# Message pass of a graph transformer block: the routing of a batch cut into eight parts over eight steps, token and gate copied per ring run, low one-hots first in VectorE's step and places last

## The reference

```python
xn = layernorm(x)
# graph attention: a softmax over the edges of each source, summed at each destination
z = leaky_relu(xn @ W_s.T [src] + xn @ W_t.T [dst]);  e = z @ W_attn.T
alpha = exp(e - m[src]) / denom[src]
agg = segment_sum(xn[src] * alpha, dst);  gnn = agg @ W_fc.T + b_fc
# linear attention over all nodes: one 64x64 matrix per head from keys and values
mix = (q @ (instance_norm(k).T @ instance_norm(v)) / N) @ w_out.T + b_out
x = x + gnn + mix
# mixture of experts, 8 experts, one expert per token, capacity C = ceil(1.25 * T / 8)
h = layernorm(x);  probs = softmax(h @ gate_w + gate_b);  idx = argmax(probs);  prb = max(probs)
pos = (running count of idx up to this token) - 1;  kept = pos < C
y = expert_mlp[idx](h) * (prb * kept);  x = x + y
```

## Time and profile before

| | us |
|---|---|
| median of 3 runs (lowest, highest) | 2184.84 (2179.74, 2191.25) |
| span of the profiled execution | 2181.3 |
| PE / DVE / ACT / POOL busy in it | 1899.4 / 1486.4 / 781.6 / 1223.5 |
| first `window_sums` of the message pass starts | 1212.19 |
| `window_sums` of step 97 starts | 1710.65 |

### The profile page before, as it was taken

The page is one execution under the profiler, slowest core; times in us unless marked ns, Lnnn a source line. Parts: engine busy times, 40 slices in busy tenths (PEclk is TensorE's granted clock), DMA queues, the critical chain, the costliest instruction groups (busy, mean ns, idle before and its releaser), DMA issues. The chain is left out here.

```text
span 2181.3 us, 44890 instructions
## 1 busy us (share of the span) xinstructions
PE 1899.4 (87%) x12055; PEld 1346.6 (62%) x12055; DVE 1486.4 (68%) x6582; ACT 781.6 (36%) x3785; POOL 1223.5 (56%) x1251
## 2 busy tenths in 40 slices
PE   8997888878888888888887899999999679999997
PEld 5654555545555545555544566666666479999996
DVE  7775788878887888788787587666767624343433
ACT  6772444444444444444443011111111123333332
POOL 0006777777777777777774576656766312222222
PEclk9997889889888899899898799889999789999998
DMA  7867888888888888888885898877978566565650
GB/s 238 245 220 208 254 243 253 248 242 242 254 245 241 251 247 250 241 253 250 246 253 165 249 313 264 266 234 254 323 245 259 157 242 200 195 202 191 204 186 28
DMA packets 287974, 507.17 MB, mean 233 GB/s; under 512 B 59024, under 2 KB 199730, under 8 KB 287580
## 3 DMA queue, kind: packets, MB, share of 16 engines
q1 hardware_dynamic: 212556, 279.91, 40.8%
q0 software_dynamic: 75152, 224.23, 34.3%
HBM read 394.78 MB, written 112.83 MB: 233 GB/s over the span
## 5 line engine op out<-in xcount | busy, mean ns | idle before, releaser
L836 POOL DMA_INDIRECT pool_mem<-node_tab,edges x592 | 580.9, 981 | 346.1 <-issue 339.7
L1659 POOL DMA_INDIRECT main<-node_tab,edges x294 | 287.6, 978 | 189.2 <-issue 81.6
L967 PE MATMUL psum<-main 32*128 32x258 f32 x1568 | 217.3, 468 | 76.9 <-DVE main L1088 73.6
L977 PE MATMUL psum<-pool_mem,ident 128*128 128x258 f32 x592 | 201.0, 469 | 34.4 <-DMA pool_mem<-node_tab,edges 34.3
L876 ACT ACTIVATE main<-score_all,neg_max 128x8 f32<-128x8 f32 x98 | 29.6, 302 | 555.0 <-DVE neg_max L1119 555.0
L836 POOL DMA_INDIRECT main<-node_tab,edges x192 | 189.5, 987 | 58.5 <-issue 54.2
L2655 POOL DMA_INDIRECT out_dram<-pool_mem x56 | 56.9, 1016 | 282.3 <-DVE pool_mem L2752 266.6
L2685 PEld LDWEIGHTS psum<-pool_mem,main 128*128 128x128 f32 x1792 | 210.9, 194 | 3.3 <-issue 0.5
L2685 PE MATMUL psum<-pool_mem,main 128*128 128x128 f32 x1792 | 211.3, 277 | 0.1
L1000 PE MATMUL psum<-wkvT,main 128*128 128x512 f32 x392 | 200.6, 637 | 7.8 <-ACT main L886 7.5
L882 ACT ACTIVATE main<-main 128x64 f32<-128x64 f32 x784 | 197.9, 334 | 24.1 <-DVE main L1133 23.6
(11 more groups left out here) (284 smaller groups left out, 3656.8 us busy)
## 6 DMA issues: line engine op xcount, KB each, us to landing
main<-in_L_ffn_w_dram SPq DMA_DIRECT2D x64, 1024.0 KB, 5.4
main<-kept_rows SPq DMA_DIRECT2D x98, 640.0 KB
kept_rows<-pool_mem SPq DMA_DIRECT2D x74, 640.0 KB, 5.5
kept_rows<-main SPq DMA_DIRECT2D x24, 640.0 KB
node_tab<-pool_mem SPq DMA_DIRECT2D x49, 258.0 KB, 3.0
main<-proj_t SPq DMA_DIRECT2D x392, 32.2 KB
pool_mem<-node_tab,edges POOLq DMA_INDIRECT x592
moe_in<-zeros SPq DMA_DIRECT2D x32, 258.0 KB, 3.8
```

The lines of the kernel that those rows point to most:

```text
L836: g.indirect_dma_start(source_rows(r, u, ZW + D), None, node_tab, bass.IndirectOffsetOnAxis(ap=edges[:, 0, HALF * k + u:HALF * k + u + 1], ...
L967: mm = pe.matmul(psum[:, Z_BANK[q], 0:ZW], hot_T[h][rows_q, j * P:(j + 1) * P], t_win[rows_q, h, :], start=True, stop=(pair in BY_VECTOR), ...
L977: pe.matmul(psum[:, Z_BANK[u % GROUPS_W], 0:ZW], ident[:, :], source_rows(r, u, ZW), start=False, stop=True).then_inc(s_z, 1)
L1659: g.indirect_dma_start(rows_g[k % R3][:, u - KEEP, 0:n], None, node_tab, bass.IndirectOffsetOnAxis(ap=edges[:, 0, HALF * k + u:HALF * k + ...
```

## The change

- `route_choice` is cut into 3 parts and `route_slots` into 5. For the first five batches (`paced`) the choice's parts stand in rounds 7, 7 and 8 and the slots' parts in 10, 11, 12, 13 and 14, one each; `rank` on PE moves from 8 to 9; `send` on POOL starts at 14 and not at 10. The last three batches keep their rounds (8, 10, 10), with all parts in one round.
- Tokens and gates are copied into `hrow` with one pair of copies for a run of tiles that lie behind one another in the ring (`runs_of`): 9 pairs in all and not 49. A `send` now waits for the whole run.
- Within `route_slots` the count for the next batch (`new_part`, `new_seen`) and other independent instructions stand between dependent ones.
- VectorE's step begins with `lows(k + 2)`; then `alphas(k + 1)`, `weights(k + 1)`, and `places(k)` behind them.

```diff
@@ -1386,7 +1386,9 @@
         BATCHES = len(SIZES)
         STARTS = [sum(SIZES[:b]) for b in range(BATCHES + 1)]
         BATCH_OF = [b for b in range(BATCHES) for _ in range(SIZES[b])]
-        LAST_STEP = HALVES + 10 + 2 * SIZES[-1]
+        SENT_PACED, SENT_LAST = 14, 10
+        CHOICE_PARTS, SLOT_PARTS = 3, 5
+        LAST_STEP = HALVES + SENT_LAST + 2 * SIZES[-1]
         XS = 12
         HR = 14
         H_RING = 2
@@ -1462,7 +1464,25 @@
 
         def sent_at(k):
 
-            return [STARTS[b] + k - 10 - SIZES[b] - 2 * STARTS[b + 1] for b in range(BATCHES) if 0 <= k - 10 - SIZES[b] - 2 * STARTS[b + 1] < SIZES[b]]
+            first = [2 * STARTS[b + 1] + SIZES[b] + (SENT_PACED if paced(b) else SENT_LAST) for b in range(BATCHES)]
+            return [STARTS[b] + k - first[b] for b in range(BATCHES) if 0 <= k - first[b] < SIZES[b]]
+
+        def paced(b):
+
+            return b < BATCHES - 3
+
+        def routed(k, offset, compact):
+
+            return [b for b in range(BATCHES) if 2 * STARTS[b + 1] + SIZES[b] + (offset if paced(b) else compact) == k]
+
+        def runs_of(b):
+
+            cut = (STARTS[b] // HR + 1) * HR
+            return [(STARTS[b], min(cut, STARTS[b + 1])), (cut, STARTS[b + 1])] if cut < STARTS[b + 1] else [(STARTS[b], STARTS[b + 1])]
+
+        def runs_to(t):
+
+            return sum(first <= t for b in range(BATCHES) for first, _ in runs_of(b))
 
         def batch_logits(b):
 
@@ -1661,7 +1681,7 @@
                                                      element_offset=ZW).then_inc(s_half[k % R3], 16)
 
                     def send(t):
-                        wait(g, s_rows_done, 2 * t + 2)
+                        wait(g, s_rows_done, 2 * runs_to(t))
                         g.indirect_dma_start(moe_in, bass.IndirectOffsetOnAxis(ap=slot_out[:, t:t + 1], axis=0), hrow[:, t % HR, :],
                                              None).then_inc(s_sentw[t % HR], 16)
 
@@ -1929,7 +1949,7 @@
                             turn(t)
                         for t in tile_at(k, 5):
                             logit(t)
-                        for b in tiled(k, 8):
+                        for b in routed(k, 9, 8):
                             rank(b)
                     count_tokens(pe)
                 with pe.Else():
@@ -2092,53 +2112,68 @@
                         dve.then(v.tensor_reduce(red_n, logits_n, AX.X, ALU.max))
                         v.tensor_tensor(logits_n, logits_n, wide(red_n), ALU.subtract).then_inc(s_r, 1)
 
-                    def route_choice(b):
+                    def route_choice(b, part):
...
-                        wait(v, s_re, b + 1)
...
+                        if part == 0:
+                            wait(v, s_re, b + 1)
+                            dve.then(v.tensor_reduce(red_n, expos_n, AX.X, ALU.add))
+                            dve.then(v.reciprocal(red_n, red_n))
+                            dve.done(v.tensor_tensor(expos_n, expos_n, wide(red_n), ALU.mult))
+                        elif part == 1:
+                            dve.wait()
+                            dve.then(v.tensor_reduce(prob_n, expos_n, AX.X, ALU.max))
+                            dve.then(v.tensor_tensor(tmp_n, expos_n, wide(prob_n), ALU.not_equal))
+                            dve.done(v.scalar_tensor_tensor(out=tmp_n, in0=tmp_n, scalar=float(NE), in1=ids(n), op0=ALU.mult, op1=ALU.add))
                         else:
-                            dve.done(v.tensor_copy(seen, new_seen))
-                            v.tensor_tensor(chosen_n, wide(expert_n), ids(n), ALU.is_equal).then_inc(s_r, 1)
-
-                    def route_slots(b):
+                            dve.wait()
+                            dve.then(v.tensor_reduce(expert_n, tmp_n, AX.X, ALU.min))
...
+                    def route_slots(b, part):
...
-                        wait(v, s_rm, b + 1)
-                        dve.wait()
-                        v.tensor_tensor(tmp_n, batch_places(b).rearrange("p (t e) -> p t e", e=NE), chosen_n, ALU.mult).then_inc(s_lgc, 1)
-                        dve.done(v.tensor_scalar(trash_n, count[:, STARTS[b]:STARTS[b + 1]], float(P), row_id[:, :], ALU.mult, ALU.add))
-                        wait(v, s_lgc, 2 * b + 2)
-                        dve.then(v.tensor_reduce(pos_n, tmp_n, AX.X, ALU.add))
...
-                        for i in range(n):
-                            t = STARTS[b] + i
-                            wait(v, s_h, t + 1)
-                            v.tensor_copy(hrow[:, t % HR, D:D + 1].bitcast(I32), token_b[:, i:i + 1]).then_inc(s_rows_done, 1)
-                            v.tensor_copy(hrow[:, t % HR, D + 1:D + 2], gate_b[:, i:i + 1]).then_inc(s_rows_done, 1)
+                        if part == 0:
+                            wait(v, s_rm, b + 1)
+                            dve.wait()
+                            v.tensor_tensor(tmp_n, batch_places(b).rearrange("p (t e) -> p t e", e=NE), chosen_n, ALU.mult).then_inc(s_lgc, 1)
+                            dve.done(v.tensor_scalar(trash_n, count[:, STARTS[b]:STARTS[b + 1]], float(P), row_id[:, :], ALU.mult, ALU.add))
+                            dve.done(v.tensor_scalar(expert_n, expert_n, float(SLOTS), None, ALU.mult))
+                            dve.done(v.tensor_reduce(new_part, chosen_n.rearrange("p t e -> p e t"), AX.X, ALU.add))
...
+                        else:
+                            dve.wait()
+                            for first, last in runs_of(b):
+                                ring = slice(first % HR, first % HR + last - first)
+                                cols = slice(first - STARTS[b], last - STARTS[b])
+                                wait(v, s_h, last)
+                                v.tensor_copy(hrow[:, ring, D].bitcast(I32), token_b[:, cols]).then_inc(s_rows_done, 1)
+                                v.tensor_copy(hrow[:, ring, D + 1], gate_b[:, cols]).then_inc(s_rows_done, 1)
 
...
+                        if k + 2 < HALVES:
+                            lows(k + 2)
                         if k + 1 < HALVES:
                             alphas(k + 1)
-                        if k + 2 < HALVES:
-                            lows(k + 2)
+                            weights(k + 1)
                         if k < HALVES:
                             places(k)
-                        if k + 1 < HALVES:
-                            weights(k + 1)
                         if k + 2 < HALVES:
                             hots(k + 2)
                         if 2 <= k < HALVES + 2 and k % 2 == 1:
@@ -2190,12 +2224,14 @@
                         for b in in_batch(k, 2):
                             for n in range(6, RSQRT_STEPS + 2):
                                 spread(b, n)
-                        for b in tiled(k, 10):
-                            route_slots(b)
+                        for part in range(SLOT_PARTS):
+                            for b in routed(k, 10 + part, 10):
+                                route_slots(b, part)
                         for b in tiled(k, 6):
                             route_logits(b)
-                        for b in tiled(k, 8):
-                            route_choice(b)
+                        for part in range(CHOICE_PARTS):
+                            for b in routed(k, 7 + part // 2, 8):
+                                route_choice(b, part)
                     chunk_table(v, dve, Arena(lo_hotT[0], HALF * P))
                 with v.Else():
                     dve = Steps(v, s_path3)
```

More of the change, by code:

```diff
@@ L2114, in route_slots @@
-                    def route_slots(b):
+                        if part == 0:
[8 more added lines that the diff above has]
+                            dve.done(v.scalar_tensor_tensor(out=tmp_n, in0=tmp_n, scalar=float(NE), in1=ids(n), op0=ALU.mult, op1=ALU.add))
+                        else:
+                            dve.wait()
+                            dve.then(v.tensor_reduce(expert_n, tmp_n, AX.X, ALU.min))
+                            if b == 0:
+                                dve.then(v.tensor_tensor(chosen_n, wide(expert_n), ids(n), ALU.is_equal))
+                                dve.done(v.memset(seen, 0.0))
+                                v.tensor_scalar(chosen[:, 0, :], chosen[:, 0, :], valid, None, ALU.mult).then_inc(s_r, 1)
+                            else:
+                                dve.done(v.tensor_copy(seen, new_seen))
+                                v.tensor_tensor(chosen_n, wide(expert_n), ids(n), ALU.is_equal).then_inc(s_r, 1)
```

46 lines of the change are left out of this document (21 added, 25 removed).

## The result

| | before | after |
|---|---|---|
| median of the runs (lowest, highest), us | 2183.86, 4 runs (2179.74 to 2191.25) | 2153.34, 4 runs (2138.15 to 2158.32) |
| profiled execution: its own time / span, us | not given / 2181.3 | 2158.32 / 2156.5 |
| PE / DVE / ACT / POOL busy, us | 1899.4 / 1486.4 / 781.6 / 1223.5 | 1882.2 / 1483.4 / 783.4 / 1226.0 |
| step 97 starts, us | 1710.65 | 1686.04 |

The ratio is **0.9845, with a 95% interval of 0.9807 to 0.9884**: 1.2% to 1.9% faster. Of the 24.8 us between the two spans, 24.6 are there when step 97 starts, so the gain lies in the message pass.

The account below looks back on a forecast made before the run. PE bounds the stage, losing 50.3 us to waits for VectorE's routing and late rows and to the lower clock behind them. 50.3 + 0.3 - 23.2 = 27.4 us off 2184.84 gives 2157 us, range 2132 to 2173.

Parts of the forecast that it names:

- The loss to be had back (50.3 us): Steps 28 to 97: PE's waits and lower clock beyond clean cycles and `rank`; the most better timing can give back.
- The 0.3 us at the end: Last batch's slots ahead of its sends: merged copies save 0.3 us on the path there.
- Step 29: VectorE's fullest step, spread plus the choice's third part: `lows(32)` was to be in time with 0.4 us to spare.
- Rival C: Routing waits go only in part, VectorE coming late in step 29: gain of 7 us, 2178 us; chance 0.12.
- The new wait: Step 44: POOL falls behind while sending, so PE waits 3.4 us for `lows(46)`, 5.8 us with the clock.
- the rule on VectorE's fp32 operations: GpSimd's DMA descriptors can't be written during two-port fp32 operations: the wait in step 44 could be 1.9 or 4.9 us.
- Which step the late rows reach: Late rows for half 44 were to hold VectorE in step 43, the heavy one, landing 37.2 us after step 35 starts.
- Stay near 35 us or grow: VectorE's waits for fetched rows were to do this, the longest in steps 43, 57, 71 and 85.
- How often and how dear: The wait of step 44 was to come again in 58, 72 and 86: 4 x 5.8 = 23.2 us lost.
- The new order: VectorE's step with `lows` first: takes `alphas`, 1.38 us, and late rows of that step off the look's path.
- The copies (nothing on the path): 18 copies in place of 98 free some 5 us of VectorE, nothing on the path except 0.3 us at the end.
- The prediction's 2.4 us a wait: PE's lower clock after each wait: the granted clock falls to 1.2 GHz, costing 2.4 us beside the wait itself.

Follow-up runs that it names:

- split_only: The changed kernel with VectorE's step in its old order (alphas, lows, places, weights, hots): 2153.78 us, ratio 0.9851.
- order_only: The kernel before with only VectorE's new step order (lows, alphas, weights, places, hots): 2181.39 us, ratio 0.9961.
- sends_apart: The changed kernel with the sends of the first four batches one in every second step: 2139.16 us, ratio 0.9782.
- sends_18: The changed kernel with the sends of the first five batches from round 18 on, not 14: 2139.70 us, ratio 0.9777.
- apart_old_order: `sends_apart` with VectorE's step in the old order (alphas, lows, places, weights): 2155.08 us, ratio 0.9838.
- copies_per_tile: The changed kernel with two copies for each tile (98) in place of one pair per run (18): 2152.24 us, ratio 0.9834.

## Why the prediction was right

**The loss to be had back (50.3 us), right.** The first cycle takes 62.95 us where 63.14 was forecast, and `split_only`, `order_only` and the after trace agree that the waits for `chosen` and behind the slots come of routing in one piece. From step 28 to 97, 363.6 us before, the floor by the prediction's sum is 313.3 (two clean cycles with `rank` and 41 steps: 2 x 63.14 + 179.3 + 7.7), and `sends_apart` comes down to 315.7. The 0.3 us at the end can't be told apart: 0.2 of the 24.8 us lie behind the start of step 97.

**Step 29, off by 0.9 us.** I had `lows(32)` 9.2 us into step 28, with 0.4 to spare. PE asked for it at 1358.42 - 0.51 = 1357.91, 9.6 in as forecast, and it was there 10.1 in: a wait of 0.51, with no loss of clock. I had named the two parts of the choice in step 28 as the reason why the room might be smaller; the sum left them out. Rival C was thus nearer than its text, but cost next to nothing.

**The new wait, right in place and in kind, and about in size.** Forecast for step 44: POOL at 5.27 us a step, rows in 9.3 us after the first fetch starts, `lows(46)` done 43.2 us after step 35 starts, a wait of 3.4 us and 5.8 in all. Measured: 5.29; 1413.17 - 1403.70 = 9.5 for the fetches of step 39, of which the first started at 1403.70; 1423.57 - 1381.13 = 42.4; a wait of 2.72; 12.39 - 6.70 = 5.7. `sends_18` shows the cause by taking it away. Of the rule on VectorE's fp32 operations that the prediction weighed (the Trainium skill, "SBUF — State Buffer", the box on the "DVE blocks DMA" trap), the measured wait lies between the two outcomes that it gave, 1.9 and 4.9 us, and on neither. Here fetches that lie beside 0.3 us or more of `lows` take 1.034 us on average and the rest that touch none of it 0.964 (62 and 182 of them, from 1240 us on). That looks like such a rule at 7%, but the same count in the kernel before gives 0.976 and 0.983, so no run shows that `lows` is the cause; what makes some fetches take 1.1 to 1.4 us stays open.

**Which step the late rows reach, wrong by one.** "VectorE needs them in step 43": the last wait for rows ends in step 42, for half 43, and half 44 is there in time. The rows of the steps before had already taken away VectorE's lead, and the full steps 42 and 43 did the rest. The end is the same since VectorE is busy from that wait on. "Stay near 35 us or grow" was wrong too: VectorE's waits for rows fell to 23.1, and the longest in the cycles stand in its steps 65 and 83 (2.59 and 2.54 us), not in 43, 57, 71 and 85. The parts with the later sends bring them to 30.0 by themselves (`split_only`), the order by itself to 41.9 (`order_only`); why the two together give 23.1 is open.

**How often and how dear, right only in the sum.** 4 x 5.8 = 23.2 us was forecast. From step 28 on the stage now takes 337.7 us, 24.4 above the floor of 313.3. But they are not four equal waits. Against the same steps where nothing waits (6.70, 3.48 and 5.00 us for steps 44 to 46 of `sends_18`), step 44 costs 5.7 us; steps 58 to 60, 25.4 us in place of 15.2, cost 10.2 for a wait of 2.25; steps 71 and 72 cost 5.2; steps 84 to 86, with three waits of 1 us and less, 2.8. And step 96 costs 3.5 us, 9.33 in place of 3.88 and a `rank` of 1.9; this I had not counted. The sixth batch still has its choice in one piece, and PE's wait there grew from 0.73 to 2.27 us. That makes 27.4, of which 3.2 are given back since the clean cycle itself came out 0.64 us shorter (60.58). The errors cancel, and that is luck: the sum has four waits of one size and one price, and neither is so.

**The new order, misjudged as a term.** "That takes the whole `alphas`, 1.38 us, and any late rows of that step off its path." The first half is about right where POOL keeps up (`apart_old_order`: 1.27 and 1.35 us of wait in steps 30 and 44). The second is not a gain: with sends in every step the rows come late whatever VectorE does first. Beside the wait in 58 that both have, the old order takes its waits in 42 and 70, which lets POOL recover, and the new one in 44 and 72. On that footing the order is worth 0; with the sends spread out, some 12 us.

**The copies (nothing on the path), right** as far as the interval of `copies_per_tile` tells.

The sum: forecast 27.4 us less, measured 24.8 between the spans and 30.5 between the medians. The stage's first 14 steps took 1.2 us more and the next 14 0.6 less. Among the kernels that have the changed kernel's code in steps 0 to 14, these steps took 73.9 to 78.1 us. It isn't the waits for the first `lows`: in the changed kernel and in `sends_18` they are 7.4 us alike, while PE is busy for 67.5 us in the one and 70.4 in the other. Some microseconds of any single comparison of spans are that.

What stays open: why the granted clock comes back within step 44 after a wait of 2.72 us and only in step 60 after one of 2.25. No run tells these two apart, and the pairs in the last section are no better understood. That VectorE's step of the choice and spread would be a bound by itself if POOL were faster yet was not tried.

## What to carry to other kernels

When bursts on one engine are cut up, the next late thing decides; look at once at the engine that was hidden behind them, here POOL with four DMAs in each of seven steps in a row, and spread its extra work over time: the same DMAs in every second step were worth 0.6%, and then POOL issued without a pause. An edit that measures nothing beside another may be worth its full price once a third one is made: the order of VectorE's step gave 0.4% alone, nothing beside late rows, and 0.6% after them, so leave-one-out tests belong at the end as well. For a stage with a fixed cycle, the sum of clean cycles is a better estimate of what can be had than the totals of waits, since a short wait can cost more in clock than in time.

## What was unexpected of the hardware

A wait of PE costs by no fixed price. 0.50 us in step 30 cost nothing more (look 1.32 us before and after it). 2.72 us cost another 3.0 (granted clock 0.72 over the step), and 2.25 us cost 8 (0.60 over two steps, matmuls at the 1.2 GHz level through a step in which PE waited for nothing). Nor does the length of the wait decide it. `apart_old_order` waits 1.77, 1.65, 1.70 and 1.76 us in steps 30, 44, 58 and 72, which take 6.70 us of work each; they took 10.04, 8.25, 12.53 and 8.37, at granted clocks of 0.83, 1.00, 0.64 and 1.00. The kernel before had such a pair already, steps 46 and 60, with the same work, 5.00 us, and the same wait, 2.10 and 2.09 us:

```profile
1447.35:1457.25 9.90, 7.80 (x42) 5.05 (x41) 6.33 (x50) 1.24 (x3) 6.04 (x7) 0.71 0.82 273
1523.89:1531.06 7.17, 5.08 (x43) 3.27 (x41) 6.16 (x50) 1.25 (x3) 5.34 (x7) 1.00 0.90 296
```

One of them cost 2.8 us beside itself and the other nothing. The prediction's 2.4 us a wait is an average over such cases, taken from the three waits of one cycle.

A fetch of 128 rows is issued by POOL in 0.95 us (median 0.947), and in two places its data are there 6.6 us after the start of the last of three: 1413.17 - 1406.58, at 299 GB/s in the 9.5 us from the first of the three on, and, before the change, 1489.61 - 1483.00 at 275 GB/s. It is not a constant: where VectorE waited for rows in these two kernels, they came 8.0 to 12.3 us after the start of the first of the three. After the change the first cycle moved 302 GB/s at a DMA share of 0.93, with 0.51 us of waiting in all on PE, so the transfers had room that 284 GB/s did not show.
